# Causal attention with a gated product on one core: unrolled engine programs, later sums of the first chunk, and 14 instead of 20 visits to the values in each group

## The reference

```python
x = L0_attn_x                                    # (2, 2048, 1024) float32
xn = (x - mean(x)) / sqrt(var(x) + 1e-5)
# attention: 32 query heads, 8 key/value heads of width 32, causal
q = (xn @ wq).reshape(b, s, 32, 32)
k = repeat((xn @ wk).reshape(b, s, 8, 32), 4)
v = repeat((xn @ wv).reshape(b, s, 8, 32), 4)
scores = where(causal, einsum('bihd,bjhd->bhij', q, k) * 32**-0.5, min)
s = einsum('bhij,bjhd->bihd', softmax(scores), v).reshape(b, s, 1024) @ wo
# gate: a dense layer and the two best of 8 low-rank experts
g = silu(xn @ W_base.T + b_base + 2.0 * lora_of_top_2(xn))
out = x + s * g
```

## Time and profile before

| | |
|---|---|
| median of 3 runs | 3469.17 us (3466.11 to 3469.25) |
| the profiled execution | 3466.9 us |
| its span in the profile | 3465.1 us |
| PE busy | 3311.4 us, 96% |
| DVE busy | 1887.9 us, 54% |
| ACT busy | 1448.7 us, 42% |
| POOL busy | 1357.7 us, 39% |
| `attend`, roughly | 668 to 2690 us |

### The profile page before, as it was taken

One profiled execution on the slowest core, in us unless ns is written; L12 is line 12 of the kernel. 1 busy time (PEld: TensorE's weight loads), 2 busy tenths in 40 slices (PEclk: granted clock), 3 DMA queues, 4 the chain that ended last, 5 costly groups with the idle time before them and its releaser, 6 DMA issues. The chain is left out here.

```text
span 3465.1 us, 54971 instructions
## 1 busy us (share of the span) xinstructions
PE 3311.4 (96%) x18048; PEld 2203.3 (64%) x18048; DVE 1887.9 (54%) x4622; ACT 1448.7 (42%) x2658; POOL 1357.7 (39%) x549
## 2 busy tenths in 40 slices
PE   6999999799999999999999999999999799989999
PEld 5888888555555555555545555555553688878887
DVE  6333332487767767767766767767772322223333
ACT  3121211156656656656655656656665211110000
POOL 0000000056766766676676676667667000000000
PEclk9999999899999999999999999999999899999999
DMA  6555554445656656556555565656655444445554
GB/s 225 164 159 165 178 166 134 116 102 119 142 112 137 131 126 132 121 127 137 125 123 129 129 134 121 137 118 133 137 136 131 157 154 140 142 134 180 192 192 174
DMA packets 283519, 494.67 MB, mean 143 GB/s; under 512 B 40864, under 2 KB 156576, under 8 KB 263328
## 3 DMA queue, kind: packets, MB, share of 16 engines
q1 hardware_dynamic: 260256, 333.04, 32.5%
q0 software_dynamic: 20736, 151.00, 21.8%
q10 hardware_dynamic: 2304, 7.87, 0.6%
HBM read 205.03 MB, written 134.74 MB: 98 GB/s over the span
## 5 line engine op out<-in xcount | busy, mean ns | idle before, releaser
L902 POOL TENSOR_TENSOR added<-added,probs 128x2048 f32<-128x2048 f32 (+3 forms) x320 | 1184.1, 3700 | 848.7 <-PE o_ps L973 814.8
L1081 DVE TENSOR_REDUCE row_max<-rows_ps 128x1 f32<-128x512 f32 x1536 | 994.3, 683 | 269.7 <-PE rows_ps L935 267.8
L1055 ACT ACTIVATE probs<-cols_ps 128x512 f32<-128x512 f32 x1728 | 927.3, 611 | 354.9 <-PE cols_ps L1017 317.7
L1085 DVE CUSTOM_DVE_ANT_0 masked_rows<-rows_ps,tri 128x128 bf16<-128x128 f32 (+3 forms) x1024 | 485.4, 483 | 236.1 <-PE rows_ps L935 203.5
L935 PE MATMUL rows_ps<-k_st,q_st 96*128 96x512 f32 (+3 forms) x1536 | 538.1, 379 | 44.0 <-DVE row_max L1085 17.4
L1017 PE MATMUL cols_ps<-q_st,k_st 97*128 97x512 f32 x1248 | 522.5, 425 | 0.6
L973 PE MATMUL o_ps<-probs,v_st 128*32 128x512 f32 (+3 forms) x4224 | 433.0, 527 | 0.0
L1017 PE MATMUL cols_ps<-q_st_last,k_st 97*128 97x512 f32 x928 | 390.1, 434 | 3.8 <-ACT dma_added L1055 2.1
L935 PEld LDWEIGHTS rows_ps<-k_st,q_st 96*128 96x128 f32 x1536 | 302.2, 197 | 143.8 <-DVE row_max L1081 47.6
L935 PE MATMUL rows_ps<-k_st,q_st_last 96*128 96x512 f32 (+3 forms) x1024 | 374.6, 390 | 7.7 <-DVE row_max L1085 4.1
L1017 PEld LDWEIGHTS cols_ps<-q_st,k_st 97*128 97x128 f32 x1248 | 238.5, 191 | 171.5 <-issue 109.5
(11 more groups left out here) (113 smaller groups left out, 3820.0 us busy)
## 6 DMA issues: line engine op xcount, KB each, us to landing
dma_added<-probs POOLq DMA_DIRECT2D x144, 1024.0 KB, 7.5
q_st<-scratch_q_hi SPq DMA_DIRECT2D x96, 256.0 KB, 5.6
x_sb<-in_x SPq DMA_DIRECT2D x32, 512.0 KB, 4.1
scratch_xt_hi<-xt_hi SPq DMA_DIRECT2D x32, 512.0 KB, 6.0
scratch_xt_lo<-xt_lo SPq DMA_DIRECT2D x32, 512.0 KB, 6.7
scratch_q_hi<-out_hi SPq DMA_DIRECT2D x64, 256.0 KB, 2.5
scratch_q_lo<-out_lo SPq DMA_DIRECT2D x64, 256.0 KB, 2.9
l_sb<-scratch_l_inv SPq DMA_DIRECT2D x256, 64.0 KB, 5.5
```

The lines of the kernel that those rows point to most:

```text
L902: nc.gpsimd.tensor_tensor(total[:, :, q0:CH], total[:, :, q0:CH], probs_of(c, j)[:, :, q0:CH], ALU.add).then_inc(pool_added, 1)
L1055: nc.scalar.activation(probs_of(c, j)[:, :, i * P:(i + 1) * P], cols_ps[cols_slot(AT_T[t])][:, :].rearrange("p (h q) -> p h q", h=NREP), A ...
L1081: nc.vector.tensor_reduce(into, bank[:, :], AX.X, ALU.max).then_inc(rows_free, 1)
L1085: nc.vector.tensor_tensor_reduce(masked_rows[rows_slot(k)][:, 0:keys], bank[:, 0:keys], tri[:, CH - keys:CH], 1.0, MASKED, ALU.add, ALU.ma ...
```

## The change

It touches three things.

1. `over_stages` with its loops is gone. All engines use the form that PE and ACT had, renamed: 16 groups written out, with constants where register values stood. The number of DVE rows in the program goes from 1676 to 3530, of POOL from 250 to 500, of SP from 548 to 909; PE goes from 8073 to 8023.
2. `PER_VISIT = 2` gives way to a list of visit sizes for each chunk: 2+2, 2+2+4, 2+3+3+4 and 2+3+3+4+4 key tiles, 14 visits. A visit stands where its last key tile puts it.
3. The sum of chunk 0 stands at the visit of key tile 2 of chunk 1 instead of key tile 0, which is 8 tiles later, and the six steps of its norm move with it.

```diff
-PER_VISIT = 2
-NVG = NJG // PER_VISIT
+VISIT_SIZES = [[2, 2], [2, 2, 4], [2, 3, 3, 4], [2, 3, 3, 4, 4]]
+VISITS = [[list(range(sum(v[:n]), sum(v[:n + 1]))) for n in range(len(v))] for v in VISIT_SIZES]
+V_OFF = [sum(map(len, VISITS[:c])) for c in range(CPB + 1)]
+NVG = V_OFF[CPB]
...
 def weighed_at(c, j):
 
-    return tiles_through(c, j - j % PER_VISIT + PER_VISIT - 1) + VISIT_AFTER - 1
+    return tiles_through(c, VISITS[c][visit_of(c, j) - V_OFF[c]][-1]) + VISIT_AFTER - 1
...
-    for _j in range(0, TPC * (_c + 1), PER_VISIT):
-        event(weighed_at(_c, _j), "W", _c, _j)
-    event(weighed_at(_c, _j) + 2, "O", _c)
+    for _steps in VISITS[_c]:
+        event(weighed_at(_c, _steps[0]), "W", _c, _steps)
+    event(weighed_at(_c, _steps[0]) + 2, "O", _c)
...
-    _t = weighed_at((_c + 1) % CPB, 0) + (0 if _c + 1 < CPB else NTG)
+    _t = weighed_at((_c + 1) % CPB, 0 if _c else 2) + (0 if _c + 1 < CPB else NTG)
     event(_t, "Y", _c)
...
-        def over_stages(engine, run):
-
-            for c in range(PEEL):
-                run(Step(0, 0), c, [op for op in FIRST_STAGES[c] if not of_group_before(op)])
-            with engine.Fori(0, NPAIR - 1) as pair:
...
-        def over_stages_once(run):
+        def over_stages(run):
...
-            over_stages(sp, run)
+            over_stages(run)
...
-            over_stages(pool, run)
+            over_stages(run)
...
-                pe.wait_ge(probs_ready, made_count(n, cc, back, j0 + PER_VISIT - 1))
-                for j in range(j0, j0 + PER_VISIT):
+                pe.wait_ge(probs_ready, made_count(n, cc, back, visit[-1]))
+                for j in visit:
...
-            over_stages(dve, run)
+            over_stages(run)
```

More of the change, by code:

```diff
@@ L559, in visit_of @@
 def visit_of(c, j):
-    return (J_OFF[c] + j) // PER_VISIT
+    return V_OFF[c] + next(n for n, steps in enumerate(VISITS[c]) if j in steps)
 EVENTS = {}
@@ L957, in _, with weigh @@
                     turn_shift(free, k, ROWS[k][1] + 1)
-            def weigh(n, cc, back, j0):
+            def weigh(n, cc, back, visit):
                 steps = TPC * (cc + 1)
                 vbuf = (n.u + back) % 2
-                if j0 == 0:
+                if visit[0] == 0:
                     if cc > 0 or not isinstance(n.pair, int) or n.pair > 0 or n.u > 0:
@@ L1025, in run @@
                         row_sums(n, *op[1:])
-            over_stages_once(run)
+            over_stages(run)
         @block.scalar
@@ L1069, in run @@
                         act.wait_ge(o_stored[cc], n.lin(16, 16 - 16 * back))
-                        act.wait_ge(values_done, n.lin(NVG, J_OFF[cc + 1] // PER_VISIT - back * NVG))
+                        act.wait_ge(values_done, n.lin(NVG, V_OFF[cc + 1] - back * NVG))
                         nc.scalar.activation(o_sb[cc][:, :], o_ps[:, :], ACT.Copy).then_inc(chunk_copied, 1)
-            over_stages_once(run)
+            over_stages(run)
         @block.vector
```

## The result

The changed kernel takes 3412.76 us (median of 4 runs, 3411.81 to 3418.56), the kernel before 3469.21 in the same comparison: a ratio of 0.9842 with the interval [0.9825, 0.9859], 56 us less. The forecast was 3404.

A forecast was written before the change was run, and what follows sets the result against it. PE was taken to bound chunk 3's window, POOL the sum of chunk 2, with DVE stalling at loop turns. Savings of 36 + 15 + 5 - 6 + 13 = 63 us took 3466.9 to 3404 us, range 3376 to 3440.

The forecast's parts named there:

- The bounds: In `attend`: PE bounds chunk 3's window, POOL's last add the sum of chunk 2, and DVE stands at loop turns.
- Part 1: Loops of DVE, POOL and SP written out: six turn windows shorten by 6.0 us each, 36 us; straight code costs nothing.
- rival D: Straight DVE code stalls where fetched; one crossing a group costing a turn's price gives 3500 us; chance 0.04.
- Part 2: Six visits fewer save 0.32 us each of width changes: 15 us in chunk 3, 5 in chunk 1, 6 lost to DVE.
- its 5 us: Chunk 1 loses one visit, under PE's bound: 0.32 us in each of 16 groups, 5 us saved.
- I take 0.4 us a group: DVE's price for longer visits: 6 us lost in all, with bounds of 0 and 2.9 us a group (46 us).
- Part 3: Later sum of chunk 0 starts and ends POOL's adds in chunk 2 0.9 us earlier: 13 us, bounds 0 and 1.8 us.
- rival C: DVE's reciprocals for chunks 1 and 2 hold its queue, 2.1 us stall twice a group: about 3510 us; chance 0.04.
- A: POOL gets out of the way at chunk 2's sum, its visits pay: 23 us more, 3381 us; chance 0.20.
- B: DVE sets the pace between longer visits, costing 46 us instead of 6: 3451 us; chance 0.14 including cases towards the forecast.
- B's sign: Chunk 3's window growing past 48.5 us, where about 47.3 instead of 47.9 was forecast.
- E: The visits don't pay because the width change is covered elsewhere: 3418 us; chance 0.58 together with the forecast.

The follow-up runs named there:

- The kernel with the late norm: Written-out kernel with late sum, two visits' key tiles each, POOL's two waits swapped, plus chunk 1's norm twelve tiles later, behind POOL's last add of chunk 2: 3381.77 us.
- small DMA adds: The kernel with the late norm, every DMA add moving one head of four: 3370.20 us with 20 visits, 3358.46 us with 17.
- lighter maxima: The kernel with the late norm, DVE taking maxima over 256 of 512 columns of full pieces: 3342.92 us with 20 visits, 3331.12 us with 14.
- 17-visit kernel: The kernel with the late norm, with only the last two visits of chunks 1, 2 and 3 joined (diagonal key tiles): 3389.91 us.
- 20 visits: Visits of two key tiles each, as before the change; written out, 3444.55 us with the early sum of chunk 0 and 3405.86 us with the late one.

## Why the total came near and its terms did not, point by point

**The bounds** were read rightly: PE between the sums, POOL at the sum of chunk 2, and DVE's stall at each turn. The kernel with the late norm shows the second: with the chain shortened the gap at the sum is gone in nine of 14 groups, and 20.3 us went with it.

**Part 1, 36 us.** The price of a turn and its mechanism held: six stalls, 37.0 us of DVE idle, and 3448.59 - 3412.76 = 35.8 us between the change and the change with its loops. What failed is that I put straight code at nothing. For DVE it is nothing: no stall stands anywhere in its written-out program, so rival D fell. This trace agrees with the Trainium skill ("Runtime: NRT & Kernel Launch", "Instruction fetch mechanics") that straight code is fetched ahead. For POOL it was not: constants where a register value stood gave each chained add a semaphore instruction of its own, 0.065 us, on the chain that sets the sum. I looked at the fetch and not at the form of the waits. And I took a window without its turn as one that leaves the next window alone: chunk 3's window grew by 0.7 us in the mean, since the clock fell behind the sum in nine groups instead of three. How these 9 us divide between POOL's slower chain and sums that a turn no longer covers isn't shown; no run had the other order of waits in the kernel that is only written out. Alone, this part gave 24.6 us.

**Part 2, 14 us.** It came out as a loss of 7 to 11 us with the late sum. The first half of the term, 0.32 us a visit, held in chunks 2 and 3 (0.33 and 0.32 with the small DMA adds) and failed in chunk 1: its 5 us came to 0.02 to 0.07 us a group. There the weight loads' waits for DVE grew from 0.2 to 0.6 us a group with the joined visit, and with the lighter maxima the window did fall, by 0.30 us. What failed is the step "I take 0.4 us a group". Take after's window of chunk 3, 48.45 us in the median, against 47.9: three visits less save 0.7 by the pair with lighter maxima (0.96 by 0.32 a visit), so the pace took 1.25 to 1.5 us a group, 20 to 24 us in all, inside my bounds of 0 to 46. I had valued a DVE that is 78% busy as a DVE with room. But a visit during which the banks run empty is followed by catching up, and there PE makes a column piece and a row piece in 0.24 + 0.24 us, faster than the 0.60 us that DVE needs for a full one. The changed kernel's PE at a visit of four full tiles:

```profile
1298.78 3.64 PE L956 MATMUL o_ps<-probs,v_st 128*32 128x512 f32 x32
...
1302.35 0.50 PE L1000 MATMUL cols_ps<-q_st_last,k_st 97*128 97x512 f32 x1
```

DVE behind it:

```profile
1303.12 1.40 DVE L1064 TENSOR_REDUCE row_max<-rows_ps 128x1 f32<-128x512 f32 x2 [2.84 <-PE rows_ps L918]
```

DVE stood 2.84 us there. I had estimated 1.3, with four full banks at the visit's start; DVE ran nearer behind PE than that. The Trainium skill ("TensorEngine Tiling (Array Packing)", "PSUM Bottleneck") says that tiling speeds TensorE and not the evacuation of PSUM, which may then bound. The pair with lighter maxima agrees as to the evacuation: what the longer visits gain in changes of width they lose on DVE's side. But what came late here were the banks of the full-width row pieces, not the output of the narrow products.

I also counted nothing for a collision of transfers. The three long windows of the changed kernel (39.1 us is shown above, with POOL's norm waiting for a DMA of SP) fit what the 17-visit kernel showed, but no run with smaller adds tried it on the changed kernel itself.

**Part 3, 13 us.** The mechanism held: the norm waits for nothing in 10 of 14 groups, the DMA add and the first add go first, and of 26 waits of DVE at the reciprocal 5 are left, so rival C fell. The size failed: 30 to 39 us by the medians instead of 13. The traces show 1.8 to 1.9 us a group, which is at my upper bound of 1.8. Of it the window that I had forecast, up to the sum of chunk 2, has 1.33 and 1.14 us instead of 0.9. I left out two things. One is the clock behind the sum: with 20 visits it fell in nine of 14 groups without the late sum and in five with it, with 14 visits in five and in three, 1.4 to 2.7 us each; that is most of the 0.50 and 0.24 us in chunk 3's window. I had read the clock at the turns only, in the earlier trace rows, and taken it as cured with them. The other is the window up to the sum of chunk 1, which with 14 visits fell by 0.43 us: there the weight loads' waits for DVE's banks fell from 1.2 to 0.6 us a group.

**The rivals.** A was right about the cause and wrong about the cure: PE's wait for POOL was worth that much, but the change leaves 0.9 us of it. The kernel with the late norm is A's case, at 3381.77 against the 3381 worked out for it, though its own sum had other parts (two visits that pay, long windows that go); the agreement of the totals is partly luck. Of B's 46 us about half came: chunk 3's window has a median of 48.45 us, just under the 48.5 named as B's sign. C and D fell. C's price was also added up wrongly: with POOL's 13 us gone they are added and not taken off, 3404 + 13 + 67 + 40 = 3524 and not about 3510. Nothing rests on it. E's time, 3418, lies nearer than the forecast's 3404, but for another reason: it took the change of width as free, and it isn't.

**The total** came out within 9 us because three errors cancelled: 11 us too much for the loops, 26 too little for the late sum, and 21 too much for the visits.

## What to carry to other kernels

An engine that is 50% busy can still set the pace where it must catch up: compare its time a piece with the producer's in that stretch, not its share of the window. When a loop is written out, look at what happens to the waits of the engine that sets the next sync point, since a second wait ahead of one instruction was an instruction more here. And once a stage is bound by a chain on another engine, take work out of that chain before anything else: one multiplication moved was worth 20 us here.

## What the runs showed of the hardware that I had not expected

- A small store on SP's queue, issued 0.6 us behind a DMA add of 1 MB, let the next step go after 8.77 us; 8.9 us behind one it took 1.48. A row of shifts issued 1.1 us behind such an add landed after 7.3 us, and PE stood for it. With adds of a quarter of the size no long window was left in 14 groups.
- In the written-out kernel the granted clock fell to its lower level behind nine of 13 waits of PE of 2.21 to 4.66 us, with 1.4 to 2.2 us lost each time; behind the other four, of 2.21 to 2.37 us, it stayed. Behind a wait of 1.83 us the window took 47.9 us.
- Two waits on constants ahead of one POOL add cost 0.065 us more than the register form of the loops, and cost nothing in the other order (gaps of 0.143, 0.079 and 0.078 us).
- A window in which PE was busy for 99% became 1.2 us shorter when DVE read half the columns. A busy share of 99% doesn't show that PE alone sets the time.
